# A pairwise-interaction tower: batch tiles of 256, 256, 512, 512, 512 rows, and steps and sums in array tiles of 64 rows by 32 columns

## The reference

```python
e = stack([tbl_f[ids[:, f]] for f in range(32)], axis=1)        # 2048 x 32 x 64
z = sum(e, axis=-1)                                             # 2048 x 32
outer = einsum('bpd,pde,bpe->bp', e[:, II], kernels, e[:, JJ])  # 2048 x 496
h = concatenate([z, outer, dense_ctx], axis=1)                  # 2048 x 544
h = relu(h @ W_top1 + b_top1)                                   # 512 wide
h = relu(h @ W_top2 + b_top2)                                   # 256 wide
y = h @ W_top3
```

## Time and profile before

| | us |
|---|---|
| median of 3 runs | 868.84 (868.46 to 869.98) |
| the profiled execution | 869.06 |
| its span, from the first to the last instruction | 867.2 |
| TensorE busy (PE) | 842.1 |
| VectorE busy (DVE) | 622.6 |
| GpSimd busy (POOL) | 483.9 |
| ScalarE busy (ACT) | 151.9 |

### The profile page before, as it was taken

One profiled execution on the slowest core, in us unless ns is written; L12 is line 12 of the kernel. 1 busy time (PEld: TensorE's weight loads), 2 busy tenths in 40 slices (PEclk: granted clock), 3 DMA queues, 4 the chain that ended last, 5 costly groups with the idle time before them and its releaser, 6 DMA issues.

```text
span 867.2 us, 15755 instructions
## 1 busy us (share of the span) xinstructions
PE 842.1 (97%) x6584; PEld 403.7 (47%) x6584; DVE 622.6 (72%) x706; ACT 151.9 (18%) x273; POOL 483.9 (56%) x518
## 2 busy tenths in 40 slices
PE   2999999999999999999999999999999999999998
PEld 1888888776645333333333333333333333333333
DVE  1776677688865888888855488888855678888850
ACT  1222312212311220120210320020111212011002
POOL 6765777777777777777776477667733430000000
PEclk9999999999999999999999999999999999999999
DMA  9511111111111111111111011111100000000000
GB/s 327 195 25 25 27 32 28 27 29 30 27 28 26 28 28 26 31 27 26 28 26 25 16 24 26 25 25 26 26 13 13 14 16 1 1 1 1 1 1 1
DMA packets 24353, 28.32 MB, mean 33 GB/s; under 512 B 13398, under 2 KB 13657, under 8 KB 24156
## 3 DMA queue, kind: packets, MB, share of 16 engines
q0 software_dynamic: 16384, 16.81, 9.8%
q1 hardware_dynamic: 7888, 10.49, 3.6%
q10 hardware_dynamic: 12, 0.01, 0.0%
HBM read 27.27 MB, written 0.01 MB: 31 GB/s over the span
## 4 chain that ended last, share of the span: by engine, by line
PE 95%; DVE 2%; DMA 1%; issue 1%; POOL 1%; ACT 0%; DVEq 0%; ACTq 0%
PE y L610 52%; PE acc L627 26%; PE y L657 5%; PE y L593 4%; PE y L685 3%; DVE prod L558 2%; PE y L668 2%; PE y L662 1%; PE y L698 1%; POOL rows L365 1%; DMA rows<-tbl,ids_sb 1%; PE y L639 0%; DMA ids_sb<-ids 0%; DVEq L259 0%; ACT h L478 0%
## 5 line engine op out<-in xcount | busy, mean ns | idle before, releaser
L558 DVE TENSOR_TENSOR prod<-y,xt 128x1024 f32<-128x1024 f32 (+2 forms) x600 | 581.8, 1031 | 198.3 <-PE y L610 197.3
L365 POOL DMA_INDIRECT rows<-tbl,ids_sb x512 | 483.2, 944 | 222.8 <-issue 112.1
L610 PE MATMUL y<-xt,kw 64*128 64x512 f32 (+2 forms) x2976 | 476.7, 462 | 4.7 <-DVE prod L558 3.5
L610 PEld LDWEIGHTS y<-xt,kw 64*128 64x128 f32 x2976 | 242.7, 189 | 219.3 <-issue 201.9
L627 PE MATMUL acc<-prod,ones_strip 128*32 128x512 f32 (+2 forms) x2976 | 239.4, 454 | 0.3 <-DVE prod L558 0.3
L627 PEld LDWEIGHTS acc<-prod,ones_strip 128*32 128x32 f32 x2976 | 79.4, 109 | 142.4 <-issue 68.1
L411 ACT COPY xt<-y 128x1024 f32<-128x1024 f32 (+3 forms) x56 | 36.2, 646 | 297.0 <-PE y L593 296.9
L593 PE MATMUL y<-ident,rows 128*128 128x128 f32 x256 | 41.2, 288 | 16.2 <-DMA rows<-tbl,ids_sb 16.1
L530 DVE TENSOR_REDUCE z_rows<-rows 128x8 f32<-128x512 f32 (+2 forms) x96 | 44.5, 497 | 15.0 <-DMA rows<-tbl,ids_sb 15.0
L442 ACT COPY h_in<-acc 128x512 f32<-128x512 f32 (+2 forms) x24 | 10.6, 443 | 240.4 <-PE acc L627 240.4
L593 PEld LDWEIGHTS y<-ident,rows 128*128 128x128 f32 x256 | 28.0, 142 | 40.8 <-issue 32.6
(11 more groups left out here) (23 smaller groups left out, 66.7 us busy)
## 6 DMA issues: line engine op xcount, KB each, us to landing
rows<-tbl,ids_sb POOLq DMA_INDIRECT x512, 2.4
kw<-pair_k SPq DMA_DIRECT2D x14, 512.0 KB, 11.4
w_sb<-w SPq DMA_DIRECT2D x1, 1024.0 KB
w_sb<-w SPq DMA_DIRECT2D x1, 512.0 KB
kw<-pair_k SPq DMA_DIRECT2D x1, 384.0 KB
kw<-pair_k SPq DMA_DIRECT2D x1, 256.0 KB, 3.9
w1z_sb<-w1z SPq DMA_DIRECT2D x1, 256.0 KB
ids_sb<-ids SPq DMA_DIRECT2D x1, 240.0 KB, 2.7
```

What stands on the lines that cost most here:

```text
L365: pool.indirect_dma_start(out=rows[:, s, c, h, :], out_offset=None, in_=tables[f], in_offset=bass.IndirectOffsetOnAxis(ap=ids_sb[:, b, f:f ...
L558: nc.vector.tensor_tensor(prod_part(t, d, n), y_part(t, d, n), x, ALU.mult).then_inc(y_read, n)
L610: last = nc.tensor.matmul(y[:, h, :], kw[part, d, :], xt[part, slot_of(t, units[h][0] // 2), 0:w], start=True, stop=True)
```

## The change

The batch is cut into five tiles of 256, 256, 512, 512 and 512 rows. In all of them (SPLIT_WIDTH is 256) each step's two matmuls of 64x128 become eight of 64x32, for four quarters of the columns. A unit's two targets are summed by two matmuls of 64x32, one on each half of the rows, and each target has a bank of its own: both banks (accs) together hold a chunk of 64 steps, so a tile has two chunks, and the first sum of a chunk waits until the chunk before it has been read. ScalarE reads both banks in one copy. The first layer's weights and h_in are ordered to fit: two chunks of two targets in place of four chunks. Everything else, the order's rules too, stays.

```diff
--- before.py
+++ after.py
@@ -8,7 +8,7 @@
 N1, N2 = 512, 256
 COUPLES = FIELDS // 2
 TILE = 512
-WIDTHS = [128, 128, 256, 512, 512, 512]
+WIDTHS = [256, 256, 512, 512, 512]
 TILES = len(WIDTHS)
 GATHER_SLOTS = 8
 XT_SLOTS = 20
@@ -17,9 +17,10 @@
 Y_SLOTS = 3
 GROUP_SLOTS = [4] * TILES
 PROD_SLOTS = 8
+SPLIT_WIDTH = 256
 SETS = COUPLES // 4
 QUADRANTS = 4
-STRIPS = 16
+STRIPS = 32
 J1, J2 = N1 // P, N2 // P
 K_CHUNKS = [2, 4, 8, 8, 8, 8, 8, 8, 8, 8, 8, 8, 8, 8, 8, 8, 6]
 
@@ -55,8 +56,8 @@
 STEPS = steps_of_tile()
 N_STEPS = len(STEPS)
 UNITS = 2 * N_STEPS
-CHUNKS = -(-N_STEPS // (2 * STRIPS))
 CHUNK_STEPS = 2 * STRIPS
+CHUNKS = -(-N_STEPS // CHUNK_STEPS)
 PAIRS = FIELDS * (FIELDS - 1) // 2
 assert sum(WIDTHS) == BATCH and 4 * UNITS // 2 >= PAIRS and sum(K_CHUNKS) == N_STEPS
 
@@ -75,6 +76,11 @@
 def pack(t):
 
     return TILE // WIDTHS[t]
+
+
+def step_columns(t):
+
+    return 32 if WIDTHS[t] >= SPLIT_WIDTH else P
 
 
 def groups(t):
@@ -270,12 +276,12 @@
         xt = sb("xt", [P, XT_SLOTS + EXTRAS, TILE])
         prod = sb("prod", [P, PROD_SLOTS, 2 * TILE])
         rows = sb("rows", [P, GATHER_SLOTS, TILE // P, 2, DIM])
-        h_in = sb("h_in", [P, CHUNKS, TILE])
+        h_in = sb("h_in", [P, CHUNKS, 2, TILE])
         z_rows = sb("z_rows", [P, TILE // P, 2, DIM])
         z_in = sb("z_in", [P, TILE])
         h1 = sb("h1", [P, J1, TILE])
         h2 = sb("h2", [P, J2, TILE])
-        w1_sb = sb("w1_sb", [P, CHUNKS, N1])
+        w1_sb = sb("w1_sb", [P, CHUNKS, 2, N1])
         w1z_sb = sb("w1z_sb", [P, N1])
         w2_sb = sb("w2_sb", [P, J1, N2])
         w3_sb = sb("w3_sb", [P, J2])
@@ -283,10 +289,10 @@
         b2_sb = sb("b2_sb", [P, J2])
         ids_sb = sb("ids_sb", [P, BATCH // P, FIELDS], i32)
         ident = sb("ident", [P, P])
-        ones_strip = sb("ones_strip", [P, 62])
+        ones_strip = sb("ones_strip", [P, 63])
 
         y_banks = [bank(f"y{i}", [P, 2, TILE]) for i in range(Y_SLOTS)]
-        accs = [bank(f"acc{i}", [P, TILE]) for i in range(2)]
+        accs = bank("accs", [P, 2, TILE])
 
         first_ids_loaded = sem("first_ids_loaded")
         ids_loaded = sem("ids_loaded")
@@ -439,7 +445,7 @@
 
                     act.wait_ge(y_full, y_use("mlp1", t - 1, 1) + 1)
                 w = WIDTHS[t]
-                nc.scalar.copy(h_in[:, c, 0:w], accs[(CHUNKS * t + c) % 2][:, 0:w]).then_inc(acc_read, 1)
+                nc.scalar.copy(h_in[:, c, :, 0:w], accs[:, :, 0:w]).then_inc(acc_read, 1)
 
             def read_fields(t):
                 u = y_use("fields", t, 0)
@@ -515,8 +521,7 @@
             dve.memset(z_rows[:], 0.0).then_inc(z_rows_zeroed, 1)
 
             dve.wait_ge(strip_zeroed, 1)
-            dve.memset(ones_strip[0:DIM, 30:31], 1.0).then_inc(consts_made, 1)
-            dve.memset(ones_strip[DIM:P, 31:32], 1.0).then_inc(consts_made, 1)
+            dve.memset(ones_strip[:, STRIPS - 1:STRIPS], 1.0).then_inc(consts_made, 1)
 
             dve.wait_ge(z_rows_zeroed, 1)
 
@@ -605,28 +610,33 @@
                     take_y(y_use("step", t, d))
                 y = y_part(t, d)
                 w = WIDTHS[t]
-                for h in range(2):
-                    part = slice(DIM * h, DIM * h + DIM)
-                    last = nc.tensor.matmul(y[:, h, :], kw[part, d, :], xt[part, slot_of(t, units[h][0] // 2), 0:w],
-                                            start=True, stop=True)
+                size = step_columns(t)
+                for first in range(0, P, size):
+                    columns = slice(first, first + size)
+                    for h in range(2):
+                        part = slice(DIM * h, DIM * h + DIM)
+                        last = nc.tensor.matmul(y[columns, h, :], kw[part, d, columns],
+                                                xt[part, slot_of(t, units[h][0] // 2), 0:w], start=True, stop=True)
                 if d % pack(t) == pack(t) - 1:
                     last.then_inc(y_full, 1)
 
             def sum_group(t, g):
                 first, end = groups(t)[g:g + 2]
                 c = CHUNKS * t + first // CHUNK_STEPS
-                acc = accs[c % 2]
-                w = WIDTHS[t]
-                if first % CHUNK_STEPS == 0 and c >= 2:
-
-                    pe.wait_ge(acc_read, c - 1)
+                w = WIDTHS[t]
+                if first % CHUNK_STEPS == 0 and c >= 1:
+
+                    pe.wait_ge(acc_read, c)
 
                 pe.wait_ge(y_read, N_STEPS * t + end)
                 for u in range(2 * first, 2 * end):
                     q, s = unit_place(u)
-                    last = nc.tensor.matmul(acc[32 * q:32 * q + 32, 0:w], ones_strip[:, 30 - 2 * s:62 - 2 * s],
-                                            prod_part(t, u // 2)[:, u % 2, :],
-                                            start=s == 0, stop=ends_chunk(t, g) and u >= 2 * end - QUADRANTS)
+                    for n in range(2):
+                        part = slice(DIM * n, DIM * n + DIM)
+                        last = nc.tensor.matmul(accs[32 * q:32 * q + 32, n, 0:w],
+                                                ones_strip[part, STRIPS - 1 - s:2 * STRIPS - 1 - s],
+                                                prod_part(t, u // 2)[part, u % 2, :], start=s == 0,
+                                                stop=ends_chunk(t, g) and u >= 2 * end - QUADRANTS)
                 last.then_inc(summed, 1)
 
             def transpose_fields(t):
@@ -654,8 +664,9 @@
                 for h in range(2):
                     j = 2 * pair + h
                     for c in range(CHUNKS - 1):
-                        nc.tensor.matmul(y[:, h, 0:w], w1_sb[:, c, j * P:(j + 1) * P], h_in[:, c, 0:w],
-                                         start=c == 0, stop=False)
+                        for n in range(2):
+                            nc.tensor.matmul(y[:, h, 0:w], w1_sb[:, c, n, j * P:(j + 1) * P], h_in[:, c, n, 0:w],
+                                             start=c == 0 and n == 0, stop=False)
                 for h in range(2):
                     part = slice(DIM * h, DIM * h + DIM)
                     j = 2 * pair + h
@@ -665,8 +676,9 @@
                 pe.wait_ge(acc_read, CHUNKS * (t + 1))
                 for h in range(2):
                     j = 2 * pair + h
-                    last = nc.tensor.matmul(y[:, h, 0:w], w1_sb[:, CHUNKS - 1, j * P:(j + 1) * P],
-                                            h_in[:, CHUNKS - 1, 0:w], start=False, stop=True)
+                    for n in range(2):
+                        last = nc.tensor.matmul(y[:, h, 0:w], w1_sb[:, CHUNKS - 1, n, j * P:(j + 1) * P],
+                                                h_in[:, CHUNKS - 1, n, 0:w], start=False, stop=n == 1)
                 last.then_inc(y_full, 1)
 
             def mlp2(t):
@@ -699,7 +711,7 @@
                                             start=c == 0, stop=c == J2 - 1)
                 last.then_inc(y_full, 1)
 
-            pe.wait_ge(consts_made, 3)
+            pe.wait_ge(consts_made, 2)
             for what, t, n in PLAN:
                 if what == "couple":
                     transpose_couples(t, n, 1)
@@ -743,7 +755,7 @@
     pair_k = np.asarray(inputs["L0_rec_kernels"])
     w_top1 = np.asarray(inputs["W_top1"])
     k = np.zeros((P, N_STEPS, P), pair_k.dtype)
-    w1 = np.zeros((CHUNKS, P, N1), w_top1.dtype)
+    w1 = np.zeros((CHUNKS, 2, P, N1), w_top1.dtype)
     for d, step in enumerate(STEPS):
         for h, (i, targets) in enumerate(units_of(step)):
             u = 2 * d + h
@@ -751,7 +763,7 @@
             for n, f in enumerate(targets):
                 pair = index[(min(i, f), max(i, f))]
                 k[DIM * h:DIM * h + DIM, d, DIM * n:DIM * n + DIM] = pair_k[pair] if i < f else pair_k[pair].T
-                w1[u // (QUADRANTS * STRIPS), 32 * q + 2 * s + n] = w_top1[FIELDS + pair]
+                w1[u // (QUADRANTS * STRIPS), n, 32 * q + s] = w_top1[FIELDS + pair]
     w1z = np.zeros((P, N1), w_top1.dtype)
     for half in (0, DIM):
         w1z[half:half + FIELDS] = w_top1[:FIELDS]
@@ -762,7 +774,7 @@
         dram_in("ids", ids),
         [dram_in(f"tbl_{f}", np.asarray(inputs[f"tbl_{f}"])) for f in range(FIELDS)],
         dram_in("pair_k", k.reshape(P, N_STEPS * P)),
-        dram_in("w1", w1.transpose(1, 0, 2)),
+        dram_in("w1", w1.transpose(2, 0, 1, 3)),
         dram_in("w1z", w1z),
         dram_in("b1", np.asarray(inputs["b_top1"]).reshape(J1, P).T),
         dram_in("w2", np.asarray(inputs["W_top2"]).reshape(J1, P, N2).transpose(1, 0, 2)),
```

## The result

The changed kernel takes 842.77 us, median of 4 runs (841.05 to 845.78); the kernel before took 868.92 beside it (868.46 to 869.98). The ratio is 0.9702, with a 95% interval of 0.968 to 0.9725: 26 us faster, and inside the range, but 16 us above the 827 that were forecast.

The account below looks back on a forecast made before the run. TensorE was taken as the bound, 95% of the chain. Span 867.2 - 17.5 - 26.4 = 823.3 us; 1.86 beyond the span gave 825.2, 2 for small waits 827.2, 0.2 off for the median: 827 us, range 818 to 858.

Parts of the forecast that it names:

- One array tile for steps and sums: TensorE, 512-row tiles: same array time, no shape change between steps and sums, groups 5.15 us instead of 5.49; -26.4 us.
- The slower rival: TensorE: eight array tiles do not run at once; with one weight load exposed each round, about 1030 us; chance 0.14.
- the rule that the prediction weighed: Trainium skill on TensorE: a weight load overlaps running matmuls only where its row group differs; by it, 1030 us.
- The 256-row tile: Second batch tile: 4.8 us saved on array shapes, 5.4 added for wider layers inside it; 103.3 us against 102.7.
- "It fits" under *Program: TensorE's instruction fetch: one more 16 KB packet, about 1.0 us, each 3.3 us in a new 256-row tile; costed at nothing.
- the rival's steady 0.236 a round: 256-row tiles: rounds take 0.236 us instead of 0.216, adding 15 us, 842 us in all; chance 0.11.
- The first tile: First 256-row tile: TensorE idles for gathered rows until about 50 us, then needs 69.5 us, ending at 119.5.
- the 6 us put down as the worst: First tile's slow start: at worst twelve steps, those of couples 6 and 7, push couple 8 back by 6 us.
- eight blocks of one couple at 0.4, three double ones and the fields at 0.6: First tile after step 27: TensorE's time for these blocks, added to 97 steps at 0.648 us and 0.7 for a copy.
- The division into tiles: Batch cut with two 256-row tiles replacing 128, 128, 256: second tile ends at 222.8 instead of 240.27, -17.5 us; 13 by itself.
- three small rivals: Rounds of 0.236, 842 us (0.11); VectorE late, 841 us (0.08); gap not one of shape, 856 us (0.04); together 0.23.
- the read of both sum banks: A chunk's first sum waits for ScalarE's 1.01 us read; costed at nothing, 9 us if fully late at all nine hand-overs.

Follow-up runs that it names:

- two equally fast kernels with other field sums: Changed kernel with VectorE's field sums cut to two values of one block, 843.63 us; changed kernel with in-group couples' field sums put behind the group's last multiplication, 843.45 us.
- changed kernel with late field sums: Changed kernel with field sums of couples inside a group put behind its last multiplication: 843.45 us, ratio 0.9708; on another chip 1274.82 us, ratio 1.0995.

## Why the prediction was right or wrong

**One array tile for steps and sums: right.** A group of the 512-row tiles takes 5.15 us, as worked out, rounds of 0.429 and no exit or entry between steps and sums. The slower rival, that eight tiles don't run at once, fell, and with it the rule that the prediction weighed: here weight loads do hide behind matmuls of their own row group (32 records with their loads, 107 ns each, in 1.72 us). That the gap is one of shape is shown from both sides, 5.51 us when only the columns differ and 5.45 when only the rows do. The term was -26.4 and is -24.0. Of the 2.4, 0.9 is in seven groups whose steps took 3.50 to 3.62 us: their fourth step waited for VectorE, whose first multiplication began 0.1 to 0.2 later than in the others. The prediction had put that margin at 0.2 and it was used up there; why VectorE began late was not followed. The rest stays open.

**The 256-row tile: a term mis-sized.** For the second tile 103.3 us were forecast and 106.7 measured (108.4 and 110.2 in the two equally fast kernels with other field sums). Within its streams of 64x32 records some 3.4 us go beyond rounds and waits for VectorE. The failed step is "It fits" under *Program*: the packet's 1.0 us was held against 3.3 us, while the blocks come 3.45 to 4.13 us apart, 3.77 on average, where TensorE waits for them. It was not the rival's steady 0.236 a round: undisturbed rounds are 0.215, and the loss sits in stops, the long ones at the blocks' boundaries.

**The first tile: the largest miss.** 119.5 was forecast, 129.6 measured. Step 27 came at 52.4 where it was to come at 50.7: +1.7, a quarter of the 6 us put down as the worst. Behind it 77.2 us passed instead of 68.8; the terms as written add up to 68.5 (62.9 and 5.6), so 8.7 are to be explained. The failed step is "eight blocks of one couple at 0.4, three double ones and the fields at 0.6": the blocks had been costed without the wait for a bank behind them. With the changes of shape around them and the waits for VectorE behind them they took 11.2 us where the prediction had 5.6, and 2.6 of the 11.2 stand one bank after the block, in mid stream, mostly where the profile's rows don't name them. Some 1.9 us more are stops and hesitations in the streams, less than in the second tile. The last 1.2 are sums: 97 steps were counted with their own sums, but by the written order those of 104 steps fall into this stretch.

**The division into tiles: right in sign, for a reason that it did not give.** The prediction gave 13 us of the gain to it whatever became of the array tiles. Alone it brings nothing (1.0009). A part of the 13 was booked wrongly: the first tile's 97 steps at 0.648 hold the gain of the array tiles already, 4 us against the old 0.69, so that by the prediction's own numbers the division alone was worth 8 to 9. The rest went into the first tile, which took 132.6 us with the old array tiles where some 124 would have been left for it, by the same waits as above. What it won against two narrow tiles, 5.0 us, the wider layers inside the second tile cost again (108.2 for 102.7). Its worth, 15 us, lies in what it spares the array tiles: twice the records for the sums of a 128-row tile, and stops for want of instructions.

**Luck in the number.** The result lies in the range because the range took in three small rivals, two of them at 841 and 842. It wasn't any of the three that came: the 16 us are made of terms that had no rival, the blocks of the first tile and the supply of instructions.

**Costed at nothing and found so:** the read of both sum banks. The chain and the waits show no wait of TensorE for ScalarE's L448. The first layer takes what it took. VectorE has 2% of the chain, below the 5% that would have spoken against the prediction.

## What to carry to other kernels

When TensorE alternates between two array tiles every few microseconds, read the gaps between groups against those inside them: here 6% of a group went into changing shape, and it came back by giving both kinds of work one shape, at the same array time, only when rows and columns both agreed. The price of small array tiles is the number of instructions; work out for each stretch how long a block of 256 lasts, compare it with the distance of blocks in a dense stretch and not with the time of one packet, and split only where the moving side is wide. Time such a kernel on more than one chip: on one here the same split made it 10% slower. A gain that is the sum of two parts should be tested part by part: here the parts gave 10 us and nothing by themselves, and 26 together.

## What the runs showed of the hardware

- TensorE received its instructions in blocks of 256, no faster than one in 3.3 us in any trace looked at (3.30 the shortest distance, in the changed kernel with late field sums), 3.77 on average in a stretch bound by them; without gathers on the other queues they still came 3.4 to 4.4 apart. A stop is named "issue" and stands in mid stream.
- A change of array tile between steps and sums cost 0.34 us a group (64x128 and 128x32), 0.36 (columns alone, 64x128 and 64x32) and 0.30 (rows alone, 64x32 and 128x32); between equal tiles nothing showed.
- Eight tiles of 64x32 ran fully side by side at 512, 256 and 128 columns: rounds of 0.429, 0.215 and 0.109 us, each with eight weight loads. Only the last didn't hold for a whole group: the 128 records of one group's sums took 2.25 us, where 16 rounds of 0.109 are 1.74; why some rounds were longer was not followed.
- TensorE started a step 0.147 us after the VectorE multiplication that freed its bank had ended.
- After a stop the tiles drift apart, and the records of steps and sums, which the program has one after the other, start mixed, as in the rows at 236.28 and 236.44 us above: four records of the new tile's steps, then four of the old one's sums.
